# Gate rows laid out in four quadrants of 32 partitions, and one wait for four PSUM banks ahead of each batch of spreading products

## What is computed

```python
x = x + conv_ref(ln_c(x), conv_w, conv_b)      # ln_c(x) * sigmoid(3x3 conv of its channel max and mean)
t = to_tokens(x)                               # (16, 12544, 64)
n = ln_t(t)                                    # LayerNorm over the 64 channels
probs = softmax(n @ router_w + router_b)       # 8 experts
top_p, top_i = top_k(probs, 2); top_p /= top_p.sum()
out = t + sum over the two chosen experts of top_p * (n @ expert_w[e] + expert_b[e])
```

## Time and profile before

| | |
|---|---|
| median of 3 runs | 1438.6 us |
| profiled execution, its own time | 1439.05 us |
| its span | 1437.3 us |
| PE busy | 1348.2 us, 94% |
| DVE busy | 1243.6 us, 87% |
| POOL busy | 1067.9 us, 74% |
| ACT busy | 1045.9 us, 73% |
| DMA | 59.6% of 16 engines |

### The profile page before, as it was taken

How to read it: one execution, slowest core, us unless ns; L and a number is a source line. 1 busy time by engine, 2 the same in 40 slices (tenths; PEclk the granted TensorE clock), 3 DMA queues, 4 the chain that set the end, 5 groups by cost and what they waited for, 6 DMA issues and landing times.

```text
span 1437.3 us, 33101 instructions
## 1 busy us (share of the span) xinstructions
PE 1348.2 (94%) x11750; PEld 631.9 (44%) x11750; DVE 1243.6 (87%) x1527; ACT 1045.9 (73%) x3949; POOL 1067.9 (74%) x659
## 2 busy tenths in 40 slices
PE   8864999999999999999999999999999988999998
PEld 8853444444444444444444444444444322333332
DVE  6786799978998899988999889988998898987776
ACT  6666888878888788878888888888888333443432
POOL 5334787887788787887787777886878886887765
PEclk9955999999999999999999999999999998999999
DMA  6442466656667666566667666576665555556563
GB/s 222 135 119 65 142 193 206 196 185 208 196 192 217 186 202 209 174 212 193 193 181 213 187 208 198 172 229 190 198 207 155 154 154 144 164 171 189 170 190 116
DMA packets 85877, 259.97 MB, mean 181 GB/s; under 512 B 13776, under 2 KB 13776, under 8 KB 85712
## 3 DMA queue, kind: packets, MB, share of 16 engines
q1 hardware_dynamic: 85712, 257.85, 59.6%
HBM read 206.42 MB, written 51.38 MB: 179 GB/s over the span
## 4 chain that ended last, share of the span: by engine, by line
PE 66%; DVE 14%; issue 8%; POOL 2%; ACT 2%; DVEq 0%; POOLq 0%; ACTq 0%
PE moe L551 38%; PE gb L497 13%; DVE gx L693 10%; PE tm L476 8%; PE tm L490 2%; PE moe L545 2%; PE tm L536 2%; PE tm L575 1%; DVE u L778 1%; DVE oh L728 1%; POOL dl L1215 1%; DVE ot L706 1%; ACT gs L980 1%; ACT sq L942 0%; POOL parts L1171 0%
## 5 line engine op out<-in xcount | busy, mean ns | idle before, releaser
L551 PE MATMUL moe<-gx,wc 128*64 128x448 f32 x3584 | 813.8, 554 | 0.0
L693 DVE TENSOR_TENSOR gx<-gb,xd 128x896 f32<-128x896 f32 x672 | 710.6, 1085 | 101.2 <-PE gb L497 97.2
L1165 POOL TENSOR_TENSOR gx<-gs,xd 128x896 f32<-128x896 f32 x224 | 489.3, 2185 | 269.0 <-ACT gs L980 213.8
L980 ACT ACTIVATE gs<-gb 128x896 f32<-128x896 f32 x224 | 205.4, 917 | 219.7 <-PE gb L497 218.7
L942 ACT ACTIVATE sq<-xct 112x64 f32<-112x64 f32 x1400 | 338.1, 244 | 7.6 <-DVE early_s L680 2.1
L551 PEld LDWEIGHTS moe<-gx,wc 128*64 128x64 f32 x3584 | 218.5, 136 | 233.0 <-issue 200.8
L497 PE MATMUL gb<-s,cg 52*128 52x448 f16 x1792 | 259.4, 357 | 42.1 <-DVE gx L693 34.4
L942 ACT ACTIVATION_READ_ACCUMULATOR sq<-xct 112x1 f32 x1400 | 263.3, 188 | 0.0
L1181 POOL TENSOR_TENSOR tt<-xc,a1s 128x896 f32<-128x896 f32 x112 | 236.2, 2109 | 11.2 <-issue 9.5
L497 PEld LDWEIGHTS gb<-s,cg 52*128 52x128 f16 x1792 | 56.8, 94 | 378.0 <-DVE gx L693 316.8
L476 PEld LDWEIGHTS tm<-rhs,xa 64*112 64x112 f32 x2800 | 170.8, 182 | 32.7 <-issue 19.0
(11 more groups left out here) (94 smaller groups left out, 1094.7 us busy)
## 6 DMA issues: line engine op xcount, KB each, us to landing
xd<-in_x_dram SPq DMA_DIRECT2D x448, 224.0 KB, 4.0
xa<-in_x_dram SPq DMA_DIRECT2D x112, 448.0 KB, 4.5
xc<-in_x_dram SPq DMA_DIRECT2D x112, 448.0 KB, 4.8
out_dram<-ot SPq DMA_DIRECT2D x112, 448.0 KB, 3.6
gx<-in_const_g_dram SPq DMA_DIRECT2D x1, 384.0 KB, 4.8
cf<-in_const_f_dram SPq DMA_DIRECT2D x1, 333.5 KB, 2.8
gx<-in_L_ffn_expert_w_dram SPq DMA_DIRECT2D x1, 128.0 KB, 4.6
cf<-in_L_ffn_expert_b_dram SPq DMA_DIRECT2D x8, 2.0 KB
```

What stands on the lines that cost most here:

```text
L551: last = pe.matmul(moe[b * CH:(b + 1) * CH, c, 0:HALF], wc[:, k * CH:(k + 1) * CH], gx[:, u, b, :], start=False, stop=(k == KT - 1), skip_ ...
L693: dve.tensor_tensor(gx[:, i, :, :], gb[:, 2 * slot:2 * slot + 2, 0:HALF], xd[:, v % 2, :, c * HALF:(c + 1) * HALF], ALU.mult).then_inc(sca ...
L980: act.activation(gs[:, j, :, :], gb[:, 2:4, 0:HALF], ACT.Copy).then_inc(gate_out, 1)
L1165: pool.tensor_tensor(gx[:, ND + j, :, :], gs[:, j, :, :], xd[:, v % 2, :, j * HALF:(j + 1) * HALF], ALU.mult).then_inc(scaled_p, 1)
```

## The change

An image's 64 rows become two quadrants of 32 rows. Each quadrant holds a copy of all 18 fp16 values, and below them the remainders of 14 columns: columns 0 to 13 in the first copy, 4 to 17 in the second. The 8 scaled gates stand at columns 4 to 11, so both copies have them with their remainders. A spread reads only the quadrant of its slot (`slot`): the four products of a batch read the rows 0, 64, 32 and 96 onward, 32 each, where they read 52 rows from 0 and 64 before. The waits for both slots of a batch stand ahead of its first product. ACT writes 576 elements per partition in `part_one` in place of 416, POOL 448 in `rest_one` in place of 416, and the scaled gates are made by one POOL instruction in place of two. `spread_a1` and `biases` contract 128 rows in place of 116. The bias is loaded by 12 DMAs of 4 rows in place of 8 of 8 rows.

```diff
+QUAD = 32
+B_LO = 4
+QG, QB_HI, QA, QM = B_LO, B_LO + E, 2 * E, 2 * E + 1
+BLOCK, AGAIN = QUAD - QN, QG
+def rows_of(b, copy, col):
+    base = b * SB + copy * QUAD
+    low = col - AGAIN * copy
+    return [base + col] + ([base + QN + low] if 0 <= low < BLOCK else [])
...
+            for b in range(2):
+                col = bias_c + b * CH
+                for n, row in enumerate(sum(bias_rows(b), [])):
+                    e = n % 2 * B_LO
+                    sp.dma_start(cf[row:row + B_LO, col:col + CH], expert_b[e:e + B_LO, :]).then_inc(ld_bias, 16)
...
             def spread(v, k, c, slot):
                 for b in range(2):
-                    rows = slice(b * SB, b * SB + 2 * PN)
+                    rows = slice(b * SB + slot * QUAD, b * SB + (slot + 1) * QUAD)
                     last = pe.matmul(gb[:, 2 * slot + b, 0:HALF], cg[rows, k * P:(k + 1) * P],
                                      s[rows, v % 2, c * HALF:(c + 1) * HALF], start=True, stop=True)
...
                     if cur:
-                        spread_for_dve(r, v, 1)
-                        spread_for_pool(r, v, 1)
+                        slot_of_dve_free(r, v, 1)
+                        slot_of_pool_free(r, v, 1)
+                        spread_for_dve(v, 1)
+                        spread_for_pool(v, 1)
...
                     if cur:
-                        spread_for_dve(r, v, 2)
-                        spread_for_dve(r, v, 3)
+                        slot_of_dve_free(r, v, 2)
+                        slot_of_dve_free(r, v, 3)
+                        spread_for_dve(v, 2)
+                        spread_for_dve(v, 3)
...
                     if cur:
-                        spread_for_dve(r, v, 4)
+                        slot_of_dve_free(r, v, 4)
                     if ahead:
-                        spread_for_pool(r, v + 1, 0)
+                        slot_of_pool_free(r, v + 1, 0)
+                    if cur:
+                        spread_for_dve(v, 4)
+                    if ahead:
+                        spread_for_pool(v + 1, 0)
...
                     if cur:
-                        spread_for_dve(r, v, 5)
+                        slot_of_dve_free(r, v, 5)
                     if ahead:
-                        spread_for_dve(r, v + 1, 0)
+                        slot_of_dve_free(r, v + 1, 0)
+                    if cur:
+                        spread_for_dve(v, 5)
+                    if ahead:
+                        spread_for_dve(v + 1, 0)
...
-                act.activation(part_of(v, 0), q_blocks(v), ACT.Copy).then_inc(part1, 1)
+                act.activation(quadrants(v)[:, :, :, 0:QN], q_blocks(v, 0, QN), ACT.Copy).then_inc(part1, 1)
...
-                pool.tensor_tensor(part_of(v, 1), q_blocks(v), part_of(v, 0), ALU.subtract).then_inc(rest1, 1)
+                pool.tensor_tensor(quadrants(v)[:, :, :, QN:QUAD], q_blocks(v, AGAIN, BLOCK), high_again(v),
+                                   ALU.subtract).then_inc(rest1, 1)
...
-                pool.tensor_tensor(q_tokens[:, rows, 0:G_LO], q_tokens[:, rows, QB:QB + G_LO], rhos[:, :, 0:G_LO],
-                                   ALU.mult).then_inc(b_pool, 1)
-                pool.tensor_tensor(q_tokens[:, rows, QB + E:QA], q_tokens[:, rows, QB + G_LO:QB + E],
-                                   rhos[:, :, G_LO:E], ALU.mult).then_inc(b_pool, 1)
+                rhos = rho[:, rows].unsqueeze(2).unsqueeze(3).to_broadcast([W, H, 2, B_LO])
+                pool.tensor_tensor(q_tokens[:, rows, QG:QG + E].rearrange("w n (i e) -> w n i e", i=2),
+                                   bias_cols(rows), rhos, ALU.mult).then_inc(b_pool, 1)
```

More of the change, by code:

```diff
@@ L81, with bias_col, bias_rows @@
 GUESS = 0x5F3759DF
[L84 to L91, removed]
+def bias_col(e):
+    return e if e < B_LO else E + e
+def rows_of(b, copy, col):
+    base = b * SB + copy * QUAD
+    low = col - AGAIN * copy
+    return [base + col] + ([base + QN + low] if 0 <= low < BLOCK else [])
+def bias_rows(b):
+    low = [0 if e < B_LO else 1 for e in range(0, E, B_LO)]
+    plain = [rows_of(b, 0, bias_col(e))[0] for e in range(0, E, B_LO)]
+    plain += [rows_of(b, c, bias_col(e))[1] for e, c in zip(range(0, E, B_LO), low)]
+    return plain, [rows_of(b, 1, bias_col(e))[0] for e in range(0, E, B_LO)]
 def constant_arrays():
@@ L111, in constant_arrays @@
     f[:, o + P] = 1.0
[L112 to L117, removed]
-    g = np.zeros((P, (KT + 2) * P), np.float32)
[L119 to L126, removed]
+    for b in range(2):
+        f[rows_of(b, 1, QM), o + b * CH:o + (b + 1) * CH] = -1.0
+        for row in bias_rows(b)[1]:
+            f[row:row + B_LO, o + P], f[row:row + B_LO, o + P + 1] = -1.0, 1.0
+    g = np.zeros((P, (KT + 2) * P), np.float32)
+    for b in range(2):
+        for copy in range(2):
+            for e in range(E):
+                lo = e // 2 * P + e % 2 * CH
+                g[rows_of(b, copy, QG + e), lo:lo + CH] = 1.0
+        g[rows_of(b, 1, QA), KT * P + b * CH:KT * P + (b + 1) * CH] = 1.0
     g[:, (KT + 1) * P:] = np.eye(P)
@@ L165, in gated_expert_program @@
         wc = sb("wc", [P, KT * CH])
-        bh = sb("bh", [SR, P], F16)
-        bw = sb("bw", [SR, P], F16)
+        bh = sb("bh", [P, P], F16)
+        bw = sb("bw", [P, P], F16)
         cwb = sb("cwb", [W, 18])
@@ L340, in stats_at, with quadrants, high_again, q_blocks @@
             return (early_s if n < EARLY else stats), 2 * ROWS * n
[L342 to L347, removed]
+        def quadrants(v):
+            return parts[:, v % 2, :, :].rearrange("w j (i k) -> w (j i) k", k=QUAD) \
+                .rearrange("w (t c) k -> w t c k", c=2)
+        def high_again(v):
+            high = parts[:, v % 2, :, :]
+            return bass.AP(high.tensor, high.offset,
+                           [high.ap[0], [2 * QUAD, 2 * ROWS], [QUAD + AGAIN, 2], [1, BLOCK]])
+        def q_blocks(v, stride, n):
             rows = q[:, v * ROWS:(v + 1) * ROWS, :]
-            return bass.AP(rows.tensor, rows.offset, [rows.ap[0], [QN, 2 * ROWS], [AGAIN, 2], [1, BLOCK]])
+            return bass.AP(rows.tensor, rows.offset, [rows.ap[0], [QN, 2 * ROWS], [stride, 2], [1, n]])
         p_int, e_int = p[:, :].bitcast(mybir.dt.int32), e[:, :].bitcast(mybir.dt.int32)
@@ L536, in spread_a1 @@
                         last = pe.matmul(tm[b * CH:(b + 1) * CH, c, 0:HALF],
-                                         cg[0:SR, KT * P + b * CH:KT * P + (b + 1) * CH],
-                                         s[0:SR, v % 2, c * HALF:(c + 1) * HALF], start=True, stop=True)
+                                         cg[:, KT * P + b * CH:KT * P + (b + 1) * CH],
+                                         s[:, v % 2, c * HALF:(c + 1) * HALF], start=True, stop=True)
                 last.then_inc(a1_spread, 1)
@@ L1184, in own, with bias_cols, halves @@
                 b_done(pool, r, B_POOL, name)
+            def bias_cols(rows):
+                cols = q_tokens[:, rows, 0:QA]
+                return bass.AP(cols.tensor, cols.offset, [cols.ap[0], [QN, H], [QB_HI, 2], [1, B_LO]])
+            def halves(t, rows):
+                return t[:, rows, :].rearrange("w n (i e) -> w n i e", i=2)
             def logits_scaled(r, h):
@@ L1223, in summed_gates @@
                     pool.wait_ge(rest1, count)
-                pool.tensor_tensor(q_tokens[:, rows, QB:QB + E], lg[:, rows, :], dl[:, rows, :], ALU.add) \
-                    .then_inc(b_pool, 1)
+                pool.tensor_tensor(bias_cols(rows), halves(lg, rows), halves(dl, rows), ALU.add).then_inc(b_pool, 1)
             def scaled_gates(r, h):
```

30 lines of the change are left out of this document (13 added, 17 removed).

## The result

| | before | after |
|---|---|---|
| median | 1439.14 us (4 runs, 1438.05 to 1440.72) | 1428.68 us (4 runs, 1426.05 to 1430.22) |
| profiled execution, span | 1439.05, 1437.3 us | 1428.17, 1426.4 us |
| one round of three phases | 164.15 us | 161.65 us |
| PE busy, share of the span | 94% | 91% |

The ratio is 0.9925, 95% interval 0.9906 to 0.9943. The kernel is faster, by 10.5 us where 21.1 were forecast. The time lies outside the forecast's likeliest range (1410 to 1426) and inside the wide one (1403 to 1453).

What follows compares the result with a forecast made beforehand. PE was taken as the bound (66% of the chain of waits). From 1439.05 us, six rounds x (5.4 - 0.6 - 0.8) = -24.0, phase C alone +1.5, start +1.4 gave 1417.95, forecast 1417.5; range 1410 to 1426, wide 1403 to 1453.

Steps and rivals of the forecast that it cites:

- The failed step: PE-bound half steps in three-phase rounds: two batches each save 0.18 to 0.19 us, so 5.62 falls to 5.24 us.
- 5.4 gross: Saving per three-phase round: 12 half steps x 0.38 = 4.6 us, plus about 0.8 from four with little DVE idle time.
- ACT and locks: Costs per three-phase round: 0.6 us for ACT's later copies, 0.8 us for DVE's longer locks behind POOL.
- ACT's tie: ACT's copy of `s` would end just when centring on PE needs it: 0.6 us per round, between 0 and 2.
- The wait: Both slots' waits before batches 1 and 3: not binding while centring is there; 1.5 us slower with phase C alone.
- The dear end: Upper bound of the wait's cost with phase C alone: 52 half steps x 0.19 = 10 us.
- The start: Four more DMAs in SP's queue delay the load of step 2: +1.4 us, at least 0.
- The remainder, ACT, POOL: ACT's `part_one` +0.13 us, POOL's remainder +0.07 us; scaled gates in one instruction between -0.5 and +0.5 us, taken as 0.
- The lock: Rival, steps 5 and 6: POOL's gap closes, DVE's piece waits through more POOL instructions; +1.8 us per round, 1452; chance 0.27.
- Pair after pair: Rival: the four quadrants do not overlap four deep, batches stay at 0.55 us, total 1452 us; chance 0.10.
- The gain is eaten: Rival: the four products overlap only in part, or ACT's tie costs 2 us per round; 1434 to 1438 us; chance 0.15.
- slow products: PE's eight experts' products after a stall, 3.25 us where 1.66 is usual; priced at 1.6 us per round.

Runs made afterwards that it cites:

- e12: Changed kernel, centring over 32 channels per image instead of 64 and ACT copying only half the tokens of `s` and `a1s`: 1478.80 us, ratio 1.0287.
- e8: Kernel before, pair after pair, spreads cut to 32 of their 52 rows from rows 0 and 64: 1458.77 us, ratio 1.0144.
- e11: Changed kernel, centring over 32 channels per image instead of 64, the other half left out: 1417.56 us, ratio 0.9857.
- e13: e12 with POOL also waiting at two places until DVE's router pieces `ge` and `dl` are done: 1405.25 us, ratio 0.9762.
- e4: Changed kernel, ACT copying only half the tokens of `s` and `a1s`: 1425.76 us, ratio 0.9914.
- e2: Changed kernel with the waits of before, each in front of its own slot's products: 1425.56 us, ratio 0.9911.
- e1: Kernel before with only the change's waits, both slots' ahead of each batch, 52-row pairs kept: 1440.87 us, ratio 1.002.
- e3: Kernel before with four of its eight bias loads split in two, 12 in all: 1438.88 us, one execution.
- e10: Kernel before with POOL waiting at two more places until DVE's router pieces `ge` and `dl` are done: 1430.84 us, ratio 0.9951.

## Why the prediction was right and wrong

**The failed step: "A half step holds two batches, so PE's half step falls from 5.62 to 5.24."** It took the batch's saving of 0.19 us twice. The saving per batch is right: 0.48 to 0.30 in the chain, 0.55 to 0.37 in the timeline. But one of the two batches stands ahead of `centre_rows`, and its saving is spent there: 1.25 us for batch and centring before, 1.26 to 1.29 after, half step 5.44 to 5.46. Where nothing stood behind it (e12), the half step did come to 5.22. The second pair of 52-row products had covered the loads of centring's weights (from 0.20 us after the batch's first load on), and 32-row products don't: e8 puts them in without the gain and pays 0.19 us, e11 puts centring in the same row tile and gets them back. The trace of before had what was needed: the earlier trace rows shows centring behind the batch, and the load that starts under the batch is one line of PE's timeline (846.12, under e8), which the forecast does not use. The question "what did the removed time cover" was put to ACT, and not to PE's own loads.

**In numbers per round.** The forecast had 5.4 gross, less 1.4 for ACT and locks: 4.0. The changed kernel gained 2.5. With the row tiles alike 1.65 more comes (e11, 160.00), and with ACT's copies halved on top 0.84 more (e13, 159.16): 5.0 in all, near the gross 5.4. ACT's tie was taken at 0.6 and is worth 0.2 behind the row tiles (e4), 0.84 without them. The six rounds thus gave -14.3 in place of -24.0. That is 9.7 of the 10.2 us by which the profiled execution (1428.17) is above the sum (1417.95); round 8, the start and phase C alone make up the rest (+0.7, +0.2, -0.4).

**The wait.** "So the wait does not bind while centring is there": right, in the rounds e2 and the changed kernel differ by 0.03 us. With phase C alone +1.1 measured, +1.5 forecast. The forecast's 26 steps with phase C alone took in ten of round 8, where phase B still runs; by the step lengths only 16 have C alone. The dear end, 10 us for pairs that stay pairs, is near what e1 paid: 7.0 us in those 16 steps (0.46 each against 0.38) and 2.4 in round 8 beside the missing stall.

**The start.** +1.4 forecast, +1.6 measured, and e3 gives it without the rest of the change, in one execution. The load of step 2 itself came 1.0 us later. Nothing later absorbed it.

**The remainder, ACT, POOL.** ACT's first part went from 546 to 678 ns (+0.13 as forecast), POOL's remainder from 965 to 1033 (+0.07 as forecast). The one instruction for the scaled gates shows no cost in any round.

**The lock.** It was given 0.27 for coming in each round, and did not come: the gap before POOL's unit shrank from 0.90 to 0.51 us and did not close, and DVE's piece took 1.88 us where it had taken 1.58. POOL and DVE of the changed kernel, against the earlier trace rows:

```profile
846.53 2.45 POOL L1191 TENSOR_TENSOR gx<-gs,xd 128x896 f32<-128x896 f32 x1 [0.51 <-ACT gs L1006]
```
```profile
845.09 1.88 DVE L741 TENSOR_TENSOR ge<-lg,top 112x896 bf16<-112x896 f32 x1
```
Its condition, three half steps below 16.1 us, fits: they stayed at 3 x 5.46 = 16.4, and at 3 x 5.22 = 15.7 in e12 the stall was there in every round. Its price was too small, 5.8 against 11.5 us per round (170.7 in e12, 159.16 in e13, which differ only in the two places): PE stands twice per round and not once, and after each time it runs at the lower clock through centring as well as the experts (see the last section). Had every half step fallen to 5.24, as the failed step has it, the rival would probably have come in and made the kernel slower than before. That is argued from e12, which also halves ACT's copies, and not shown: e11, where half of the centrings stay at 0.99, reached rounds of 160.00 without a stall, with a gap of 0.53 us left in POOL's work. The forecast and this rival were closer to one case than their separate chances say.

**Pair after pair** is out, by the 0.37 us of a batch. The Trainium skill, "TensorE: Matmul & The Clock Gate", section "Measured speedup vs the span model", has 3.07 times for four row tiles. Here four take 0.37 us where one takes 0.36, so 3.9 times. The span model of the same section, the length of one product and about 4 ns for each further tile, gives 0.37 and agrees. **The gain is eaten** came nearer with its time (1434) than the forecast did, but not by its mechanism: the overlap is not partial, and ACT takes 0.2 us per round and not 2.

## What to carry to other kernels

When a product gets shorter, read PE's weight loads beside its stream: what the old product covered comes back as time, above all where the next group works on another number of rows. Put a price on each place of a repeated saving by what follows it there, not on the half step as a whole. And where DVE's two-input operations live between POOL's instructions, work out the gap that POOL has left at the new speed; an ordering wait on POOL cost little here (two of them left five rounds of e10 as they were and made one 0.3 us longer) and took the stall away.

## What the hardware showed that was not expected

*The row tile.* Going from 32-row products to 64-row products costs 0.19 us here, in e8 with nothing but the number of rows changed: the next loads start when the last products are nearly through (0.48 us after the batch's first load, against 0.20 to 0.29). The Trainium skill, "TensorEngine Tiling (Array Packing)", section "Key Properties", says that changing the tiling mode drains TensorE. The traces fit that, and put a price on it. Products of 52 rows followed by products of 64 rows pass without it (centring 0.77 in the earlier trace rows). The step from centring to the 128-row experts shows no difference between the kernels (eight experts' products take 1.65 to 1.66 us in the chain, behind centring over 64 rows and over 32).

*The lock's hand-over.* DVE's piece, 1.30 us at its shortest, took 6.46 to 7.12 us while POOL's instructions followed each other, so, behind the instruction that it found running, it lost two turns in a row (in e12 POOL's L1193 and L1210, 881.87 to 886.05) or three (in round 8), and not one. With a gap of 0.51 us it took 1.88. Who wins at a hand-over no run here settles; what the runs show is that a wait which holds POOL until DVE is done (e10, e13) takes the stall away.

*After such a stall PE runs at the lower clock.* PE had been idle for 5.23 us in e12, and what it did next took nearly twice as long: in the timeline the eight experts' products 3.26 us where 1.72 is usual there, centring 1.64 where it is 0.92. It is the granted clock, which is 1.00 before the gap (868 to 886) and 0.50 behind it, the lower of its two levels, 1.2 and 2.4 GHz (columns as in the earlier trace rows):

```profile
888.00:893.00 5.00, 4.94 (x28) 2.56 (x28) 4.74 (x6) 1.79 (x10) 0.00 (x0) 0.50 0.40 102
```

From this batch to the next are 5.10 us where 2.70 is usual, so the stall's price is its length and 2.4 us more, and some 0.4 in the stretch behind. The second gap of the round, 3.06 us, is followed by the same clock and the same 5.10 us. In round 8 of the kernel before the clock is 0.50 from 1186 to 1190 too, which is where the forecast's "slow products" come from.
